# One-hots of the first edge pass kept in DRAM and loaded again in layer two's pass of a graph network

## The reference, cut to what matters

```python
# block 0 (layer k=0): mean over incoming edges
agg = segment_sum(h[src], dst) / max(count, 1)
x = x + relu(h @ W_self.T + agg @ W_neigh.T + bias)
# block 1 (k=1): product over incoming edges of h[src] * edge_feat * filter(dist) * cutoff
x = x + ssp(segment_prod(msg, dst) @ W3 + b3)
# block 2 (k=2, 3, 4): three mean layers
msg_sum = segment_sum(x[src], dst)
mean = msg_sum / max(count, 1)
x = mean @ W_agg[i] + x @ W_root[i] + b[i]      # relu after the first two
# block 3 (k=5, 6, 7): three attention layers, each with a batch norm
```

## Time and profile before

| what | value |
|---|---|
| median of 3 runs | 8200.4 us (8199.71 to 8201.25) |
| the profiled execution | 8196.53 us, span 8194.7 us |
| TensorE busy | 5086.2 us (62%) |
| VectorE busy | 5183.9 us (63%) |
| ScalarE busy | 2016.9 us (25%) |
| GpSimd busy | 4885.3 us (60%) |
| one-hots of the first pass (L1917) | 98, begun between 53.4 and 1034.0 us |
| one-hots of layer two's pass (L1917) | 98, begun between 2261.0 and 3492.4 us |
| mean granted TensorE clock | 0.72 of full speed |

### The profile page before, as it was taken

How to read it: one execution, slowest core, us unless ns; L and a number is a source line. 1 busy time by engine, 2 the same in 40 slices (tenths; PEclk the granted TensorE clock), 3 DMA queues, 4 the chain that set the end, 5 groups by cost and what they waited for, 6 DMA issues and landing times.

```text
span 8194.7 us, 105099 instructions
## 1 busy us (share of the span) xinstructions
PE 5086.2 (62%) x25856; PEld 3340.8 (41%) x25856; DVE 5183.9 (63%) x17135; ACT 2016.9 (25%) x3703; POOL 4885.3 (60%) x5045
## 2 busy tenths in 40 slices
PE   5665556666557777789999883542573542754532
PEld 3444443333333334444444442542443532434532
DVE  7787567777668888820000196862696853797745
ACT  6666653444425565520000100000100000000000
POOL 6777747777566666600000177777677776677774
PEclk8777767777677777799999955765656765656756
DMA  6555556777424455578788623421223421234321
GB/s 178 164 156 155 155 157 196 205 198 203 132 89 178 176 189 181 182 256 291 270 302 290 224 75 117 119 75 37 77 89 117 122 58 35 79 114 123 94 52 32
DMA packets 728927, 1217.08 MB, mean 149 GB/s; under 512 B 109340, under 2 KB 547085, under 8 KB 714832
## 3 DMA queue, kind: packets, MB, share of 16 engines
q1 hardware_dynamic: 552716, 847.76, 31.0%
q0 software_dynamic: 161120, 311.32, 14.6%
q10 hardware_dynamic: 14688, 53.48, 1.7%
HBM read 865.31 MB, written 346.85 MB: 148 GB/s over the span
## 4 chain that ended last, share of the span: by engine, by line
POOL 49%; PE 21%; issue 20%; DVE 7%; ACT 1%; DVEq 1%; DMA 1%; SPq 0%; POOLq 0%; ACTq 0%
POOL RO L997 27%; POOL RO L967 18%; PE PS L1505 13%; PE PS L1462 3%; PE PS L1442 3%; POOL nd L980 2%; POOL at_first L973 2%; DVE acc L1941 1%; DVE shared L2056 1%; DVE cut_row L2056 1%; DVE bn L2055 1%; ACT H L1122 1%; POOL acc L1014 1%; ACT PS L1123 0%; PE PS L1349 0%
## 5 line engine op out<-in xcount | busy, mean ns | idle before, releaser
L997 POOL DMA_INDIRECT RO<-table,src_t x2346 | 2244.2, 957 | 1997.9 <-DMA table<-H 1247.1
L967 POOL DMA_INDIRECT RO<-table,src_t x2346 | 2298.5, 980 | 1100.5 <-issue 729.3
L1941 DVE TENSOR_TENSOR acc<-acc,PS 128x128 f32 x3910 | 1107.0, 283 | 1061.7 <-PE PS L1545 748.7
L1545 PE MATMUL PS<-RO 128*128 128x128 f32 x3060 | 689.6, 416 | 1165.5 <-DMA RO<-table,src_t 1141.9
L1545 PEld LDWEIGHTS PS<-RO 128*128 128x128 f32 x3060 | 636.9, 317 | 1210.1 <-DMA RO<-table,src_t 1188.4
L2156 DVE TENSOR_SCALAR RO<-PS,loc_t,shared 128x128 f32<-128x128 f32 x2346 | 953.1, 408 | 0.3
L1462 PE MATMUL PS<-RO 128*128 128x128 f32 x3128 | 647.0, 392 | 391.7 <-DMA RO<-table,src_t 376.5
L1462 PEld LDWEIGHTS PS<-RO 128*128 128x128 f32 x3128 | 618.6, 300 | 478.6 <-DMA RO<-table,src_t 454.2
L1122 ACT ACTIVATE H<-PS 128x392 f32<-128x392 f32 x784 | 390.7, 498 | 494.2 <-PE PS L1442 482.3
L2055 DVE TENSOR_SCALAR bn<-work,shared 128x128 bf16<-128x128 int16 x1567 | 434.1, 277 | 103.5 <-PE PS L1442 80.9
L1262 ACT ACTIVATE small<-small 128x49 f32<-128x49 f32 x3 | 0.7, 245 | 2013.3 <-DVE small L2402 2013.3
(11 more groups left out here) (382 smaller groups left out, 8604.3 us busy)
## 6 DMA issues: line engine op xcount, KB each, us to landing
GT<-adjacency SPq DMA_DIRECT2D x126, 1792.0 KB, 7.2
adjacency<-H SPq DMA_DIRECT2D x98, 1568.0 KB
RO<-adjacency SPq DMA_DIRECT2D x42, 1792.0 KB, 7.2
RO<-table,src_t POOLq DMA_INDIRECT x4692, 3.2
staged<-RO ACTq DMA_DIRECT2D x102, 512.0 KB
H<-staged SPq DMA_DIRECT2D x102, 512.0 KB, 3.7
soft_rows<-shared SPq DMA_DIRECT2D x196, 256.0 KB
H<-soft_rows SPq DMA_DIRECT2D x98, 512.0 KB, 3.9
```

Of the source, the lines that this page charges most:

```text
L967: pool.indirect_dma_start(rows[:, h * HT + j, :], None, table[k % 2], at(src_t[:, t:t + 1]))\
L997: pool.indirect_dma_start(rows[:, g % 2 * HT + j, :], None, table[k % 2], at(src_t[:, t:t + 1]))\
L1545: last = mm(PS[:, o:o + D], block[:, j * D:(j + 1) * D], onehot[:, h * HT + j, :], start=True, stop=True)
L1941: tt(at, at, window_at(k, c, j), ALU.add).then_inc(added[h], 1 if j < n - 1 else HT - n + 1)
```

## The change

96 of the 98 one-hot groups of the first pass (groups 2 to 97) are stored to a DRAM buffer `kept`, one 512 KB store each, from SP's queue behind the step's edge-weight loads. VectorE waits, before it overwrites a half of `onehot`, for the store of that half. In layer two's pass VectorE builds the one-hots of groups 0 and 1 only; SP loads the others back, each as soon as group c-2 is multiplied, and TensorE waits for that load in place of VectorE's signal. The stores of the 98 slabs move from SP's queue to ScalarE's, each behind the evacuation of the slab's last window. The counts of `onehot_ready` are adapted (`hots`). The semaphores of the stores and loads are ones that other stages use (`edges_in`, `soft_in`).

```diff
--- before.py
+++ after.py
@@ -112,6 +112,7 @@
         flat_bf = dram("flat_bf", (7, EPAD), BF16)
         soft_rows = dram("soft_rows", (P, EPAD))
         prod_rows = dram("prod_rows", (EPAD, D))
+        kept = dram("kept", (NG, P, HT * D))
         at_first = dram("at_first", (EPAD, 2))
         at_last = dram("at_last", (EPAD, 2))
         staged = dram("staged", (P, SG * GROUP_WORDS))
@@ -621,6 +622,20 @@
         table_parts = {k: (n + 1) * NCH for n, k in enumerate(GATHERED)}
 
         turn = {0: 0, 2: 1, 5: 2, 6: 3, 7: 4}
+        hots = {0: 0, 2: ITERS, 5: ITERS + 1, 6: 2 * ITERS + 1, 7: 3 * ITERS + 1}
+        onehot_kept, onehot_in = edges_in, soft_in
+
+        def kept_after(c):
+
+            return onehot_kept[c % 2], 16 * 4 + 16 * (c // 2)
+
+        def back_after(c):
+
+            return onehot_in[c % 2], 16 * ITERS + 16 * (c // 2)
+
+        def onehots_of(c):
+
+            return onehot[:, c % 2 * HT:(c % 2 + 1) * HT, :].rearrange("p t d -> p (t d)")
         pass_of = {k: n for n, k in enumerate(GATHERED)}
 
         def taken(c):
@@ -781,6 +796,9 @@
                     for p in pieces_of(c):
                         if p + DIST_SLOTS < PIECES:
                             distances(p + DIST_SLOTS)
+                    if 2 <= c < NG:
+                        sp.wait_ge(onehot_ready[c % 2], c // 2 + 1)
+                        sp.dma_start(kept[c], onehots_of(c)).then_inc(onehot_kept[c % 2], 16)
 
             def first_softs(i, h):
                 wait(sp, z_ready[1], i * 2 + h - 1)
@@ -821,11 +839,10 @@
                 sp.dma_start(table[k % 2][rows_of, :].rearrange("(t p) f -> p t f", p=P), chunk(rows3, c))\
                     .then_inc(table_stored, 16)
 
-            def store_slabs():
-                for q in range(SLABS):
-                    sp.wait_ge(evacuated, AHEAD + WN * (q + 1))
-                    sp.wait_ge(slabs_moved, 16 * (q + 1))
-                    sp.dma_start(adjacency[:, q * SLAB_WORDS:(q + 1) * SLAB_WORDS], slab(q)).then_inc(slabs_moved, 16)
+            def take_onehots():
+                for c in range(2, NG):
+                    sp.wait_ge(*multiplied_by(2, c - 2))
+                    sp.dma_start(onehots_of(c), kept[c]).then_inc(onehot_in[c % 2], 16)
                 sp.wait_ge(slabs_moved, 16 * (SLABS + 1))
 
             def load_units(k):
@@ -912,7 +929,7 @@
                     sp.wait_ge(perm_copied, PERMS)
                     sp.dma_start(perm_rows, G).then_inc(perm_stored, 16)
                 if k == 2:
-                    store_slabs()
+                    take_onehots()
                     sp.dma_start(G, perm_rows).then_inc(perm_loaded, 16)
                 if k == 1:
                     sp.wait_ge(perm_stored, 16)
@@ -1121,6 +1138,11 @@
                     bank = PS[:, bank_of:bank_of + MASKW]
                     nc.scalar.activation(to, bank.rearrange("p (h d) -> p h d", d=WN), ACT.Copy)
                     nc.scalar.activation(bank, bank, ACT.Copy, scale=0.0).then_inc(evacuated, 1)
+                    if w % WN == WN - 1:
+                        q = w // WN
+                        s.wait_ge(evacuated, AHEAD + WN * (q + 1))
+                        s.wait_ge(slabs_moved, 16 * (q + 1))
+                        s.dma_start(adjacency[:, q * SLAB_WORDS:(q + 1) * SLAB_WORDS], slab(q)).then_inc(slabs_moved, 16)
 
             def dense_layer(k):
                 done = (k - 3) * NCH
@@ -1451,7 +1473,10 @@
                 for c in range(NG):
                     h, i = c % 2, c // 2
                     pe.wait_ge(*gathered_by(k, c))
-                    pe.wait_ge(onehot_ready[h], i + 1 + turn[k] * ITERS)
+                    if k == 2 and c >= 2:
+                        pe.wait_ge(*back_after(c))
+                    else:
+                        pe.wait_ge(onehot_ready[h], i + 1 + hots[k])
                     for j in range(real_tiles(c)):
                         if j % 4 == 0:
                             windows_free(k, 2 * c + j // 4)
@@ -1535,7 +1560,7 @@
                     else:
                         pe.wait_ge(*gathered_by(k, g))
                         block = rows[:, g % 2 * HT:(g % 2 + 1) * HT, :].rearrange("p a b -> p (a b)")
-                    pe.wait_ge(onehot_ready[h], c // 2 + 1 + turn[k] * ITERS)
+                    pe.wait_ge(onehot_ready[h], c // 2 + 1 + hots[k])
                     pe.wait_ge(added[h], (c // 2) * HT + turn[k] * (ITERS * HT))
                     for j in range(real_tiles(c)):
                         if c == NG - 1 and j == LH:
@@ -1952,8 +1977,13 @@
                     if k == 0 and c > 0:
                         for p in pieces_of(c - 1):
                             first_softplus(p)
+                    if k == 0 and c == NG - 1:
+                        for b in range(2):
+                            v.wait_ge(*kept_after(NG - 2 + b))
                     add_group(k, c, c * HT)
                     if c + 2 < NG:
+                        if k == 0 and c >= 2:
+                            v.wait_ge(*kept_after(c))
                         make_onehot(k, c + 2)
                     if 1 <= c <= NCH:
                         take_product(k, c - 1)
@@ -2076,8 +2106,6 @@
                         masks_to(ended)
                     else:
                         add_group(2, c, c * HT)
-                    if c + 2 < NG:
-                        make_onehot(2, c + 2)
                     for m in chunks_beside(c - 1):
                         take_product(2, m)
                     plan(c)
```

## The result

The kernel with the change takes 8497.8 us (median of 4 runs, 8492.5 to 8504.3) beside 8200.8 us before: a ratio of 1.036, with a 95% interval of 1.0342 to 1.0378. It is slower, as forecast, but by 297 us where 42 were forecast, and 173 us beyond the high end of the range. The profiled execution has a span of 8489.6 us; before it was 8194.7, so 294.9 us are to be found in the traces.

What follows compares the result with a forecast made beforehand. The prediction took GpSimd's gathers to bound the first pass and VectorE and TensorE to tie in layer two. First pass +57, layer two -20, ScalarE +5 gave +42 us: 8242 us, range 8165 to 8325.

Steps and rivals of the forecast that it cites:

- That GpSimd sets the pace and VectorE's chain would pass it: First pass, digit steps: GpSimd's gathers took 10.2 us a group; VectorE's loop would grow from 9.1 to 11.3 us.
- The two filters take 1.96 us: First pass: time of a step's two filter matmuls on TensorE, which the edge-weight loads ahead of the store wait for.
- L = 3.4: First pass: time for the 512 KB store to land after issue, 2.6 us bare plus 0.8 behind a 256 KB load.
- My high end of 5.8: First pass: longest landing allowed for the store, 5.0 us plus 0.8, giving a 13.7 us loop and 172 us.
- D+3.2 and 3.4 to D+6.7 for the one-hot: First pass, counted from a step's first softplus: store issued at 3.2 us, landing 3.4, next one-hot at 6.7.
- Elsewhere hidden: First pass outside the digit steps: gathers hide the store's wait, with +4 us for uneven steps early on.
- the forecast's 8.9 and 9.8: First pass: forecast loops in us, 8.9 from 740 to 1060 us and 9.8 from 53 to 250 us.
- The store lands late, 8330: Rival, first pass: store lands at 5 us or more, loop 13 and up, +90 us on the forecast; chance 0.12.
- the tie of two equal paths: Layer two's pass: VectorE's one-hot and six masks take as long as TensorE's sixteen matmuls; the edit shortens only one.
- The 13 us for the masks' part: Layer two, part with masks: gain from removed one-hots, 21 of 86 groups at 0.6 us each.
- the 7 of the steps before it: Layer two, nine steps before the masks: 7 us gained, the one-hot being on the round trip in about six.
- +5 forecast: Layer two: 98 slab stores moved to ScalarE, 0.5 us each with a tenth on the path; bounds 0 and 49.

## Why the prediction missed

- **That GpSimd sets the pace and VectorE's chain would pass it:** right. So was the loop as the way to price it, and the 4.6 us from the one-hot to the next softplus.
- **"The two filters take 1.96 us":** this term failed. The step at 601.70 had them at nearly full clock (granted 0.89 from 602 to 604 us). Already in the old loop that was the short case: the four matmuls spanned under 2.2 us in 20 of 45 digit steps, 2.35 in the mean, and after the change 3.58 (a record's mean went from 709 to 1057 ns; the records overlap). The new wait makes TensorE idle longer, the clock falls to 1.2 GHz, and the filters, which free the slots of the loads ahead of the store, are late by what they take more. The price was read from one step of the old loop, though the edit changes what TensorE does before the filters.
- **"L = 3.4":** measured 4.6. The line through two transfers gave 2.6 for the bare store; ahead of the loads, with the softplus stores before it, it took 3.4 to 6.5 us and 4.4 in the mean. By the Trainium skill ("DMA: Bandwidth & Descriptors", section "Anatomy of one DMA — SWDGE (gpsimd) path") the estimate was 3.2, still under all of these but nearer than the line that I took. No run has the store with nothing ahead of it. My high end of 5.8 held the 4.6.
- **The clock and the landing aren't independent.** With the clock repaired the landing grew from 4.6 to 6.1, and the one-hot came at D+9.3 all the same. So the step that failed is the sum of the two, D+3.2 and 3.4 to D+6.7 for the one-hot, where D+9.4 was measured; the filters' 1.96 us put right alone gave back 11 us of the pass at most.
- **"Elsewhere hidden":** this failed with them. The same 2.7 us added to the forecast's 8.9 and 9.8 give 11.6 and 12.5, over the gathers' 10.8 and 10.4; 12.5 and 12.4 were measured. I had carried the high L into the steps with digits alone, so 172 us, with 6 elsewhere, was the most that I thought the pass could lose. It lost 194 in those steps and 110 elsewhere. Even that high end made the forecast 8242 + 121 = 8363, which my range, ending at 8325, left out. With slacks of 1.9 and 0.6 us outside the digits, the high L belonged into those steps too.
- **"The store lands late, 8330":** the rival with the right sign and kind. It too had the price in the digit steps only.
- **Layer two:** the tie of two equal paths was right, and the kernel with the one-hots left out shows it. The 13 us for the masks' part were 0 or less (the change lost 9.0 there), the 7 of the steps before it were 9.6. Of the 20 us 0.6 are left.
- **ScalarE:** +5 forecast, nothing to measure when moved alone. TensorE's wait for it grew by 19.5 us in the change, but the end of the pass didn't follow.

## What to carry to other kernels

A store of a buffer that is soon rewritten is priced by when its queue gets to it and when it lands, and only then by its bytes: put it ahead of everything that waits for work of the same step. When an edit lengthens a loop, price the other engines' instructions again for the loop as it will be, with the clock that TensorE has after the new idle time. And where two engines' paths tie, taking work from one of them buys nothing until the other has work to give; here moving two masks into the gap did what removing 1.2 us could not.

## What the runs showed of the hardware that I had not expected

- Few bytes don't make a quick store. A 32 KB store behind two loads lands 3.4 us after its issue in the mean of 46 steps at half clock (2.9 to 4.4), and 4.4 in the mean of 43 at full clock (3.5 to 5.6); a 512 KB store ahead of the loads takes 4.4 (3.4 to 6.5). The Trainium skill, page "DMA: Bandwidth & Descriptors", section "Queues, rings and completion order", says that a transfer's signal lands only after every earlier write of the same DMA engine, of other queues too. The short store's landing agrees with that, but no run has a 32 KB store alone, so it isn't shown apart from the engines' sharing.
- A quicker issue can be lost whole in the landing: 1.65 us earlier out, 0.16 us earlier landed, in the means of 23 steps at full and 15 at half clock of one trace; in the step shown the DMA engines were busy 0.99 and 0.93 of the time.
- One chip ran the kernel before in 10170.8 us, 24% longer than the others, with 7 runs within 0.2%. Only ratios, and only with a run of the kernel before beside them, can be read from such a chip.
